# Self attention stage: projections, weighted sums and totals moved to other slots of a group, row maxima two slots further ahead

## The chip, the cores and the metric

One Trainium2 chip, one core. The metric is device time in microseconds of one execution; a median of runs is given. The kernel is one program in which the five engines (TensorE, VectorE, ScalarE, GpSimd, SyncE) each run their own instruction list and wait for each other on semaphores only.

## The reference, cut to what matters

A decoder layer on x of 8 x 512 x 512 with 16 heads of 32: self attention with a second "memory" branch, cross attention against ctx_1024, a small two-expert feed-forward, and a layer norm behind each. The change lies in the self attention alone:

```python
qk = x @ w_attn.T + b_attn              # q and k; v = x
scores = einsum('bhqd,bhkd->bhqk', q, k) * scale   # causal
y_ar = einsum('bhqk,bhkd->bhqd', softmax(scores), v)
k2 = x[:, :-1] @ w_k2.T + b_k2
qa = -leaky_relu(-q2 * scale, 0.02);  ka = sigmoid(k2 * scale * 0.02)
# a later stage: ma = tril(qa ka^T), y_ma = ma @ (v[1:] - y_ar[:-1])
```

## The kernel before, in words

The self stage works on 32 groups (8 batches x 4 groups of 4 heads). A group has 16 slots, numbered 0 to 15 in the texts; `split_slot` gives each as (kt, j): a tile kt of 128 keys and a head j. So slot 4 is (1, 0), slot 11 is (2, 3). Every engine walks the same list of slots, and within a slot it issues what belongs to it in the order of the code. There is no planner; tables and `if` lines on (kt, j) set all of the order.

What TensorE issues in slot n of group g (`self_tensor`):

1. the transposed scores of slot n (L339; 512, 384, 256, 256 columns for kt = 0 to 3). It waits until the exponential of slot n-2 has left one of two PSUM banks, and in slot 0 for the row `self_shift`, the negated row maxima, that a DMA (L759) puts under the stacked q/k operand;
2. plain scores for the row maxima of a slot further ahead (L390 in `self_scores`, SELF_LEAD = 24 slots; 256, 256, 384, 512 columns, by m % 4). They wait for the stacked operand of the group that they belong to (`kq_landed`, the DMAs of L752) and for VectorE's maximum of three slots before (`dve_max`);
3. in slot 11 the weighted sums of key tiles 0 and 1 (L403);
4. at most one projection step: three 512-column matmuls (L203 to L205) of a later group, in 12 slots of 16, by the table PROJECTED. A group's steps are 0 to 3 for q, 4 to 7 for k, 8 to 11 for k2;
5. in slot 3 the weighted sums of tiles 2 and 3 of the group before, and then its totals (L362, into PSUM bank 6);
6. in slot 10, last, the transpose of the next group's row maxima (L378) into bank 6. It waits until VectorE has normalised the group before, which uses bank 6 as well (`dve_norm`).

VectorE in each slot takes the row maximum of slot n + SELF_LEAD (L583), then has: the low part of k (L590, slot 2), the normalisation of the group before (`self_norm`: four reciprocals of 128 columns, L620, in slots 4 to 7, and one multiplication, L626, in slot 8), the low part of the shift (L598, slot 11), and the low part of q and qa (L606, L610, slot 14). ScalarE has the exponential of every slot (L465), the copy of k (L470, slot 1), the copy of y (L483, slot 4), tanh for ka (L478, slot 6), its + 1 (L488, slot 8), a copy for the totals (L493, slot 9), the copy of the shift (L499, slot 11), and q and its relu (L507, L511, slot 13). GpSimd masks each tile's exponentials (L652) and adds them up (L668). SyncE issues all DMAs in order: the stack of 12 for the next-but-one group (L752, slot 5), v, qa, ka, and the shift (L759, slot 12). Bank 7 carries q and k2, bank 6 carries k, totals and the transpose.

Before group 0 there are three groups of slots (g = -3 to -1) in which only projections and maxima are done; group 1's q and k are projected by a second table (SECOND) in slots 1 to 8 of g = -2. From g = 29 on (LATE_NORM) the normalisation comes behind the transpose. Behind the last slot the memory stage and then the cross attention follow.

Of the kernel before, what the change touches and what calls it, by code (L numbers as in the profile page):

```python
# [16 lines left out]
P = 128  # L17
# [19 lines left out]
SELF_MAX = (0, 1, 5)  # L37
CROSS_MAX, CROSS_MAX_FIRST = (1, 0), (0, 1, 7)

SELF_LEAD, CROSS_LEAD = 24, 22  # L40


def split_slot(n):
# [12 lines left out]
def arrive(eng, sem):  # L56

    eng.drain().then_inc(sem, 1)
# [152 lines left out]
class SelfPhase:  # L211
    def __init__(self, nc, ctx, t):
        def sem(name):
# [62 lines left out]

PROJECTED = {(0, 0): (2, 7), (0, 1): (1, 8), (0, 2): (1, 9), (0, 3): (1, 10), (1, 1): (1, 11), (2, 0): (3, 0),
             (2, 1): (3, 1), (2, 2): (3, 2), (3, 0): (3, 3), (3, 1): (3, 4), (3, 2): (3, 5), (3, 3): (3, 6)}  # L280

SECOND = {(0, 1): 0, (0, 2): 1, (0, 3): 2, (1, 0): 3, (1, 1): 4, (1, 2): 5, (1, 3): 6, (2, 0): 7}
SECOND_AT = -2
Q_COPY, Q_LOW, K_COPY, K_LOW, STACK_AT = (3, 1), (3, 2), (0, 1), (0, 2), (1, 1)
SECOND_Q_COPY, SECOND_Q_LOW, SECOND_K_COPY, SECOND_K_LOW, SECOND_STACK = (1, 1), (1, 2), (2, 1), (2, 2), (2, 2)


# [31 lines left out]
def shift_bank(sh, d):  # L319

    return sh.bank[7 if d > LATE_NORM else 6]


def self_tensor(pe, s, second, third, cw, sh):
    pe.wait_ge(sh.const, CONSTS)
    pe.wait_ge(s.pool_ones, 3)
    for n in SELF_SLOTS:
        g, kt, j = split_slot(n)
        if n in ROUND_AT:
            memory_round_tensor(pe, s, second, third, cw, sh, ROUND_AT[n])  # L330
        if 0 <= n < NS:
            first = kt * P
            q0 = min(first, SEQ - 256)
            kq, bank = s.kq[g % 3], sh.bank[2 + n % 2]
            if kt == 0 and j == 0:
                pe.wait_ge(s.shift_landed[g % 3], 32 * (g // 3 + 1))
            if n >= 2:
                pe.wait_ge(s.act_exp, n - 1)
            pe.matmul(bank[:, 0:SEQ - q0], kq[0:98, 1, j, first:first + P], kq[0:98, 0, j, q0:SEQ],  # L339
                      start=True, stop=True).then_inc(s.pe_st, 1)  # L340
        m = n + SELF_LEAD
        if 0 <= m < NS:
            self_scores(pe, s, sh, m)

        if (kt, j) == (2, 3) and 0 <= g < NG:
            self_weighted(pe, s, sh, TILES * g)
            self_weighted(pe, s, sh, TILES * g + 1)
        part = projection_at(g, kt, j)
        if part is not None:
            self_project(pe, s, sh, *part)  # L350
        if kt == 0 and j == 3 and 0 <= g - 1 < NG:
            d = g - 1
            self_weighted(pe, s, sh, TILES * g - 2)
            self_weighted(pe, s, sh, TILES * g - 1)
            pe.wait_ge(s.pool_add, 3 * (d + 1))
            pe.wait_ge(s.act_copied, d + 1)
            pe.wait_ge(s.dve_k, min(d + 4, NG))
            if d + 4 > NG:
                pe.wait_ge(s.dve_sh, min(d + 2, NG))
                pe.wait_ge(s.dve_norm, NORM * d)  # L360
            for jj in range(PER):
                done = pe.matmul(sh.bank[6][rows_of(jj), :], sh.ones[:, :], s.added[:, jj, :],  # L362
                                 start=True, stop=True, skip_group_check=True)
            done.then_inc(s.pe_tot, 1)
        if kt == 2 and j == 2 and 0 <= g + 1 < NG:
            d, n16 = g + 1, PER * TILES
            pe.wait_ge(s.dve_max, n16 * (d + 1))
            if g == LATE_NORM:

                pe.wait_ge(s.act_k2, 2 * (g + 1) + 1)  # L370
            elif g > LATE_NORM:
                pe.wait_ge(s.dve_sh, g + 1)
                pe.wait_ge(s.act_k2, min(2 * (g + 1) + 1, 2 * NG - 1))
            elif g >= 1:
                pe.wait_ge(s.dve_norm, NORM * g)
            else:
                pe.wait_ge(s.dve_k, g + 3)
            pe.transpose(shift_bank(sh, d)[0:n16, 0:P], s.negmax[d % 2][:, :], sh.ident[:, :]).then_inc(s.pe_sh, 1)  # L378
    arrive(pe, sh.self_done)


def self_scores(pe, s, sh, m):
# [57 lines left out]
def self_scalar(act, s, second, third, cw, sh):  # L440
# [6 lines left out]
    for n in SELF_SLOTS:  # L447
        g, kt, j = split_slot(n)
        if g == -2 and kt == 2 and j == 2:
            for i in range(2 * GROUPS, 3 * GROUPS):  # L450
                self_weight_high(act, s, i)
        if n in ROUND_AT:
            memory_round_scalar(act, second, third, cw, sh, ROUND_AT[n])
        if 0 <= n < NS:
            step = n // PER
            first = kt * P
            q0 = min(first, SEQ - 256)
            if j == 0 and step >= 3:
                before = step - 3
                act.wait_ge(s.pe_pv, before + 1)  # L460
                act.wait_ge(s.pool_add, 3 * (before // TILES) + max(before % TILES, 1))
                if before % TILES == 0:
                    act.wait_ge(s.act_copied, before // TILES + 1)
            act.wait_ge(s.pe_st, n + 1)
            act.activation(s.pt[step % 3][:, j, 0:SEQ - first], sh.bank[2 + n % 2][:, first - q0:SEQ - q0], ACT.Exp,  # L465
                           scale=SCALE_SELF).then_inc(s.act_exp, 1)
        d = copied_at(g, kt, j, K_COPY, SECOND_K_COPY, 2)
        if d is not None:
            act.wait_ge(s.pe_k, d + 1)
            act.activation(s.stage[d % 2][:, 2, :].bitcast(F32R), sh.bank[6][:, :], ACT.Identity,  # L470
                           bias=bias_column(s, K, d)).then_inc(s.act_k, 1)
        if kt == 1 and j == 2 and 0 <= g + 1 < NG:
            d = g + 1
            ka = s.memory[:, 1, 1:SEQ]
            act.wait_ge(s.pe_k2, d + 1)
            if d >= 1:
                act.wait_ge(s.ka_stored, 16 * d)
            act.activation(ka, sh.bank[7][:, 0:SEQ - 1], ACT.Tanh, bias=bias_column(s, K2, d), scale=KSCALE).then_inc(s.act_k2, 1)  # L478
        if kt == 1 and j == 0 and 0 <= g - 1 < NG:
            act.wait_ge(s.pe_pv, TILES * g)  # L480
            if g >= 2:
                act.wait_ge(s.dve_norm, NORM * (g - 1))
            act.activation(s.y_raw[:, :], sh.bank[4][:, :], ACT.Copy).then_inc(s.act_raw, 1)  # L483
        if kt == 2 and j == 0 and 0 <= g + 1 < NG:
            d = g + 1
            ka = s.memory[:, 1, 1:SEQ]
            act.wait_ge(s.act_k2, 2 * d + 1)
            act.activation(ka, ka, ACT.Copy, bias=1.0).then_inc(s.act_k2, 1)  # L488
        if kt == 2 and j == 1 and 0 <= g < NG:
            act.wait_ge(s.pool_mask, TILES * g + 1)  # L490
            if g >= 1:
                act.wait_ge(s.pe_tot, g)
            act.activation(s.added[:, :, 0:P], s.pt[TILES * g % 3][:, :, 0:P], ACT.Copy).then_inc(s.act_copied, 1)  # L493
        if kt == 2 and j == 3 and 0 <= g + 1 < NG:
            d = g + 1
            act.wait_ge(s.pe_sh, d + 1)
            if d >= 1:
                act.wait_ge(s.shift_landed[(d - 1) % 3], 32 * ((d - 1) // 3 + 1))
            act.activation(s.shift[:, 0, :].bitcast(F32R), shift_bank(sh, d)[0:PER * TILES, 0:P],  # L499
                           ACT.Copy).then_inc(s.act_sh, 1)  # L500
        d = copied_at(g, kt, j, Q_COPY, SECOND_Q_COPY, 3)
        if d is not None:
            if d >= 2:
                for jj in range(PER):
                    act.wait_ge(s.kq_landed[(d - 2) % 3][jj], 48 * ((d - 2) // 3 + 1))
            act.wait_ge(s.pe_q, d + 1)
            act.activation(s.stage[d % 2][:, 0, :].bitcast(F32R), sh.bank[7][:, :], ACT.Identity,  # L507
                           bias=bias_column(s, Q, d)).then_inc(s.act_q, 1)
            if d >= 1:
                act.wait_ge(s.dve_q, 2 * d)  # L510
            act.activation(s.relu[:, :], sh.bank[7][:, :], ACT.Relu, bias=s.bias_relu[:, d % GROUPS:d % GROUPS + 1],  # L511
                           scale=-RELU).then_inc(s.act_q, 1)
        if next_x(g, kt, j) is not None:
            self_x_high(act, s, next_x(g, kt, j))
# [33 lines left out]
def bias_column(s, which, g):  # L548
    return s.bias[:, which * GROUPS + g % GROUPS:which * GROUPS + g % GROUPS + 1]


def self_vector(dve, s, second, third, cw, sh):
# [15 lines left out]
    for n in SELF_SLOTS:  # L568
# [3 lines left out]
                self_weight_low(dve, s, i)  # L572
        if n in ROUND_AT:
            memory_round_vector(dve, second, third, cw, sh, ROUND_AT[n])
        m = n + SELF_LEAD
        if 0 <= m < NS:
            gm, jm, qt = split_slot(m)
            if jm == 0 and qt == 0 and gm >= 2:
# [11 lines left out]
            dve.scalar_tensor_tensor(out=st[:, 3, :].bitcast(F32R), in0=sh.bank[6][:, :], scalar=bias_column(s, K, d),  # L590
                                     in1=st[:, 2, :], op0=ALU.add, op1=ALU.subtract).then_inc(s.dve_k, 1)
        if 0 <= g - 1 < NG and not LATE_NORM <= g < NG - 1:
            self_norm(dve, s, sh, g - 1, PER * kt + j - PER)
        if kt == 2 and j == 3 and 0 <= g + 1 < NG:
            d = g + 1
            hl = s.shift
# [1828 lines left out]
```

## Time and profile before

| | |
|---|---|
| median of 3 runs | 1758.37 us (1756.82 to 1758.61) |
| profiled execution | 1754.45 us, its span 1752.7 us |
| TensorE busy | 1663.1 us, 95% of the span |
| VectorE, ScalarE, GpSimd busy | 1256.1, 992.1, 1160.6 us |

The span is the time from the first to the last instruction of the profiled execution. A line of the timeline gives the start in us, the duration in us, engine, line and operation; a bracket at its end is the idle time of the engine before it and what ended it. Matmuls overlap: one with 512 columns lasts some 0.4 us but the next can start 0.23 us behind its start, so the distance of starts is what counts. "PEld" is the weight load that goes ahead of a matmul.

### The profile page before, as it was taken

The page shows a single profiled execution, that of the slowest core. Times are in us where ns is not written, and L with a number is a line of the kernel's source. Part 1 is how long each engine was busy: PE and PEld are TensorE (multiplying, and loading weights), DVE is VectorE, ACT ScalarE, POOL GpSimd, SP SyncE. Part 2 cuts the span into 40 slices and gives each one's busy share as a digit, 9 for nine tenths or more (in the row PEclk, how much of TensorE's full clock was granted, in tenths as well). Part 3 has the DMA queues.
Part 4 walks back from the last instruction along what each step waited for, and adds up shares of the span by engine and source line. Part 5 has one row for each costly group of instructions (what it writes and reads, how often), then busy time and mean ns, then how long its engine had stood idle before and what let it go on. Part 6 is the DMA issues. An engine that isn't in the chain of part 4 may idle for free.

```text
span 1752.7 us, 30880 instructions
## 1 busy us (share of the span) xinstructions
PE 1663.1 (95%) x10584; PEld 1097.7 (63%) x10584; DVE 1256.1 (72%) x2786; ACT 992.1 (57%) x2002; POOL 1160.6 (66%) x963
## 2 busy tenths in 40 slices
PE   6999999999999889999998999999999999999998
PEld 4666666666666647877863456566565655656566
DVE  6677777777777656767876786877778687777845
ACT  4555555555555543433445666666666666667564
POOL 1555556556555564745565987969788786888874
PEclk9999999999999989999998999999999999999999
DMA  7566566565555555576625543535344344534210
GB/s 216 136 156 166 140 158 163 144 157 154 155 142 150 139 172 180 186 236 186 192 71 157 146 115 88 139 95 153 91 120 115 85 133 103 140 94 117 64 43 30
DMA packets 172311, 237.80 MB, mean 136 GB/s; under 512 B 22646, under 2 KB 74102, under 8 KB 172156
## 3 DMA queue, kind: packets, MB, share of 16 engines
q1 hardware_dynamic: 172156, 235.84, 49.0%
q8 instruction: 85, 1.39, 0.3%
q14 instruction: 70, 0.57, 0.1%
HBM read 92.10 MB, written 41.94 MB: 76 GB/s over the span
## 4 chain that ended last, share of the span: by engine, by line
PE 67%; DVE 12%; POOL 7%; DMA 5%; issue 3%; SPq 3%; ACT 2%; POOLq 0%; DVEq 0%; ACTq 0%
PE bank L1698 9%; POOL cross_added L2040 5%; PE bank L1567 5%; PE bank L203 5%; PE bank L204 5%; PE bank L1535 5%; PE bank L205 5%; DVE bank L620 5%; PE bank L1506 5%; PE bank L403 4%; PE bank L339 4%; PE bank L390 3%; SPq L752 2%; DVE bank L583 2%; PE bank L1603 2%
## 5 line engine op out<-in xcount | busy, mean ns | idle before, releaser
L1516 DVE TENSOR_REDUCE cross_negmax<-bank 128x1 f32<-128x512 f32 x512 | 338.8, 675 | 132.6 <-PE bank L1506 129.1
L1785 ACT ACTIVATE cpt<-bank 128x512 f32<-128x512 f32 x512 | 297.3, 595 | 122.6 <-PE bank L1535 119.9
L583 DVE CUSTOM_DVE_ANT_0 bank<-bank,future 128x128 f32<-128x128 f32 (+3 forms) x512 | 243.2, 488 | 172.2 <-PE bank L390 171.9
L465 ACT ACTIVATE pt<-bank 128x256 f32<-128x256 f32 (+3 forms) x512 | 217.7, 445 | 261.1 <-PE bank L339 254.9
L2040 POOL TENSOR_TENSOR cross_added<-cross_added,cpt 128x2048 f32<-128x2048 f32 x61 | 280.1, 4591 | 11.4 <-ACT cpt L1785 11.0
L652 POOL TENSOR_SCALAR_AFFINE_SELECT pt<-pt 128x512 f32<-128x512 f32 x128 | 81.1, 634 | 247.0 <-ACT pt L465 246.8
L1535 PE MATMUL bank<-cqk 98*128 98x512 f32 x512 | 225.8, 441 | 10.0 <-ACT cpt L1785 9.5
L1506 PE MATMUL bank<-cqk 96*128 96x512 f32 x512 | 211.6, 417 | 11.0 <-DVE cross_negmax L1516 8.9
L2040 POOL TENSOR_TENSOR cross_added<-cpt,cpt 128x2048 f32<-128x2048 f32 x32 | 146.7, 4585 | 78.1 <-ACT cpt L1785 78.1
L339 PE MATMUL bank<-qk 98*128 98x256 f32 (+2 forms) x512 | 179.2, 355 | 10.5 <-ACT pt L465 4.9
L390 PE MATMUL bank<-qk 96*128 96x256 f32 (+2 forms) x512 | 169.1, 336 | 5.5 <-DVE self_negmax L583 4.4
L203 PE MATMUL bank<-xt_hi,w_hi 128*128 128x512 f32 x384 | 157.4, 410 | 13.0 <-DVE w_lo L541 10.8
L1535 PEld LDWEIGHTS bank<-cqk 98*128 98x128 f32 x512 | 97.0, 190 | 106.0 <-issue 51.2
L204 PE MATMUL bank<-xt_hi,w_lo 128*128 128x512 f32 x384 | 153.7, 400 | 0.0
L339 PEld LDWEIGHTS bank<-qk 98*128 98x128 f32 x512 | 96.3, 189 | 90.6 <-issue 46.9
L205 PE MATMUL bank<-xt_lo,w_hi 128*128 128x512 f32 x384 | 152.4, 397 | 0.0
L1875 DVE RECIPROCAL bank<-bank 128x128 f32<-128x128 f32 x128 | 121.8, 954 | 42.4 <-PE bank L1603 42.4
L1567 PE MATMUL bank<-cpt,cv 128*32 128x512 f32 x1024 | 138.1, 612 | 0.0
L1506 PEld LDWEIGHTS bank<-cqk 96*128 96x128 f32 x512 | 96.0, 189 | 49.8 <-DVE cross_negmax L1516 26.7
L620 DVE RECIPROCAL bank<-bank 128x128 f32<-128x128 f32 x128 | 121.8, 957 | 4.9 <-PE bank L362 4.9
L668 POOL TENSOR_TENSOR self_added<-self_added,pt 128x1024 f32<-128x1024 f32 x64 | 117.4, 1835 | 5.3
L390 PEld LDWEIGHTS bank<-qk 96*128 96x128 f32 x512 | 98.1, 192 | 26.0 <-DVE self_negmax L583 11.5
(210 smaller groups left out, 3619.9 us busy)
## 6 DMA issues: line engine op xcount, KB each, us to landing
qk<-stage SPq DMA_DIRECT2D x384, 128.0 KB, 2.4
cqk<-cstage SPq DMA_DIRECT2D x384, 128.0 KB, 2.3
scratch_memory<-memory SPq DMA_DIRECT2D x64, 256.0 KB, 3.8
ma<-scratch_memory SPq DMA_DIRECT2D x32, 512.0 KB, 4.0
raw<-in_x_t SPq DMA_DIRECT2D x32, 256.0 KB, 2.9
v<-in_x SPq DMA_DIRECT2D x32, 256.0 KB, 3.3
scratch_y_ar<-y_ar SPq DMA_DIRECT2D x32, 256.0 KB, 2.7
my_ar<-scratch_y_ar SPq DMA_DIRECT2D x32, 256.0 KB, 4.5
```

What stands on the lines that cost most here:

```text
L203: pe.matmul(out, a[0], b[0], start=first, stop=False)
L204: pe.matmul(out, a[1], b[0], start=False, stop=False)
L205: return pe.matmul(out, a[0], b[1], start=False, stop=last)
L339: pe.matmul(bank[:, 0:SEQ - q0], kq[0:98, 1, j, first:first + P], kq[0:98, 0, j, q0:SEQ], start=True, stop=True).then_inc(s.pe_st, 1)
L390: pe.matmul(bank[:, 0:max(keys, 256)], kq[0:96, 0, j, tile_of(qt)], kq[0:96, 1, j, 0:max(keys, 256)], start=True, stop=True).then_inc(s.pe ...
L583: dve.tensor_tensor_reduce(out=scores, in0=scores, in1=sh.future[:, SEQ - P * (qt + 1):SEQ], scale=-1.0, scalar=-NEG, op0=ALU.add, op1=ALU ...
L1506: pe.matmul(max_bank(sh, m)[:, :], kq[0:96, 0, jm, tile_of(qt)], kq[0:96, 1, jm, :], start=True, stop=True).then_inc(s.pe_mx, 1)
L1516: dve.reduce_max(s.negmax[gm % 2][:, col:col + 1], max_bank(sh, m)[:, :], AX, negate=True).then_inc(s.dve_max, 1)
L1535: pe.matmul(sh.bank[2 + n % 2][:, :], kq[0:98, 1, j, tile_of(kt)], kq[0:98, 0, j, :], start=True, stop=True).then_inc(s.pe_st, 1)
L1567: done = pe.matmul(sh.bank[4][rows_of(j), :], s.v[g % 2][:, kt, rows_of(j)], s.pt[step % 3][:, j, :], start=(kt == 0), stop=(kt == TILES - ...
L1785: act.activation(s.pt[step % 3][:, j, :], sh.bank[2 + n % 2][:, :], ACT.Exp, scale=SCALE_CROSS).then_inc(s.act_exp, 1)
L2040: pool.tensor_tensor(s.added[:, :, :], old[:, :, :], s.pt[step % 3][:, :, :], ALU.add).then_inc(s.pool_add, 1)
```

## The change

On TensorE: the row-maximum scores run 26 slots ahead instead of 24; the weighted sums of tiles 2 and 3 and the totals go from slot 3 to slot 4 (where there is no projection); the twelve projection steps lie in slots 0 to 3, 5 to 8 and 12 to 15 instead of 0 to 3, 5, 8 to 10 and 12 to 15, so that k ends in slot 15 and no longer in slot 0; the transpose of the maxima is in slot 11, ahead of the weighted sums, and no longer at the end of slot 10. On VectorE: the maxima run 25 slots ahead instead of 24, the normalisation one slot later (5 to 9), the low part of k in slot 1. On ScalarE: k's copy in slot 0, q's in slot 12, tanh ahead of the exponential of slot 4, its + 1 in slot 6, the copy for the totals in slot 7.

```diff
-SELF_LEAD, CROSS_LEAD = 24, 22
+SELF_LEAD, SELF_MAX_LEAD, CROSS_LEAD = 26, 25, 22
-PROJECTED = {(0, 0): (2, 7), (0, 1): (1, 8), (0, 2): (1, 9), (0, 3): (1, 10), (1, 1): (1, 11), (2, 0): (3, 0),
-             (2, 1): (3, 1), (2, 2): (3, 2), (3, 0): (3, 3), (3, 1): (3, 4), (3, 2): (3, 5), (3, 3): (3, 6)}
+PROJECTED = {(0, 0): (1, 8), (0, 1): (1, 9), (0, 2): (1, 10), (0, 3): (1, 11), (1, 1): (3, 0), (1, 2): (3, 1),
+             (1, 3): (3, 2), (2, 0): (3, 3), (3, 0): (3, 4), (3, 1): (3, 5), (3, 2): (3, 6), (3, 3): (3, 7)}
-Q_COPY, Q_LOW, K_COPY, K_LOW, STACK_AT = (3, 1), (3, 2), (0, 1), (0, 2), (1, 1)
+Q_COPY, Q_LOW, K_COPY, K_LOW, STACK_AT = (3, 0), (3, 2), (0, 0), (0, 1), (1, 1)
@@ self_tensor
+        if kt == 2 and j == 3 and 0 <= g + 1 < NG:
+            self_shift(pe, s, sh, g)
         if (kt, j) == (2, 3) and 0 <= g < NG:
             self_weighted(pe, s, sh, TILES * g)
             self_weighted(pe, s, sh, TILES * g + 1)
         part = projection_at(g, kt, j)
         if part is not None:
             self_project(pe, s, sh, *part)
-        if kt == 0 and j == 3 and 0 <= g - 1 < NG:
+        if kt == 1 and j == 0 and 0 <= g - 1 < NG:
...
-        if kt == 2 and j == 2 and 0 <= g + 1 < NG:
...
+def self_shift(pe, s, sh, g):      # the removed block, its waits unchanged
@@ self_scalar
-        if kt == 1 and j == 2 and 0 <= g + 1 < NG:     # tanh, behind the exponential
+        if kt == 1 and j == 0 and 0 <= g + 1 < NG:     # tanh, ahead of the exponential
-        if kt == 2 and j == 0 and 0 <= g + 1 < NG:     # ka + 1
+        if kt == 1 and j == 2 and 0 <= g + 1 < NG:
-        if kt == 2 and j == 1 and 0 <= g < NG:         # copy for the totals
+        if kt == 1 and j == 3 and 0 <= g < NG:
@@ self_vector
-        m = n + SELF_LEAD
+        m = n + SELF_MAX_LEAD
-            self_norm(dve, s, sh, g - 1, PER * kt + j - PER)
+            self_norm(dve, s, sh, g - 1, PER * kt + j - PER - 1)
```

## Rows read from the trace of the kernel before

**Rows 1.** The page, busy time and share of each engine.
```profile
PE 1663.1 (95%) x10584; PEld 1097.7 (63%) x10584; DVE 1256.1 (72%) x2786; ACT 992.1 (57%) x2002; POOL 1160.6 (66%) x963
```

**Rows 2.** Windows: length, busy of PE, PEld, DVE, ACT, POOL, granted clock, DMA.
```profile
28.50:35.50 7.00, 4.56 (x11) 3.51 (x12) 5.47 (x17) 0.00 (x0) 1.09 (x1) 0.51 0.89 204
300.00:600.00 300.00, 289.22 (x1729) 197.04 (x1729) 213.32 (x648) 167.42 (x388) 167.66 (x123) 1.00 0.56 149
608.00:616.00 8.00, 5.47 (x15) 4.45 (x16) 4.40 (x13) 1.81 (x4) 3.45 (x3) 0.57 0.21 64
```

**Rows 3.** Line L378: idle time before it, and who ended it.
```profile
  DVE y_ar L626: 14.4, 28
```

**Rows 4.** Timeline of TensorE, one group: slot 11 to slot 11.
```profile
301.56 0.27 PE L378 MATMUL bank<-ident,self_negmax 128*16 128x128 f32 x1 [0.52 <-DVE y_ar L626]
301.59 0.36 PE L339 MATMUL bank<-qk 98*128 98x256 f32 x1
...
302.12 1.71 PE L403 MATMUL bank<-pt,v 128*32 128x512 f32 x16
...
307.80 0.40 PE L339 MATMUL bank<-qk 98*128 98x512 f32 x1
...
308.15 0.40 PE L203 MATMUL bank<-xt_hi,w_hi 128*128 128x512 f32 x1
308.38 0.40 PE L204 MATMUL bank<-xt_hi,w_lo 128*128 128x512 f32 x1
...
312.27 0.86 PE L403 MATMUL bank<-pt,v 128*32 128x256 f32 x16
312.95 1.04 PE L362 MATMUL bank<-self_added,ones 128*32 128x512 f32 x8
...
314.20 0.28 PE L390 MATMUL bank<-qk 96*128 96x256 f32 x1
...
320.46 0.27 PE L378 MATMUL bank<-ident,self_negmax 128*16 128x128 f32 x1 [0.52 <-DVE y_ar L626]
```

**Rows 5.** Timeline of VectorE in the same group, behind the totals.
```profile
314.52 0.30 DVE L583 CUSTOM_DVE_ANT_0 bank<-bank,future 128x128 f32<-128x128 f32 x1 [2.09 <-PE bank L390]
314.74 0.96 DVE L620 RECIPROCAL bank<-bank 128x128 f32<-128x128 f32 x1
...
319.63 0.68 DVE L626 TENSOR_TENSOR y_ar<-bank,self_y_raw 128x512 f32<-128x512 f32 x1
...
321.74 0.27 DVE L598 TENSOR_TENSOR self_shift<-bank,self_shift 16x128 fp32r<-16x128 f32 x1
```

**Rows 6.** Timeline, stack and shift: VectorE's low part of k, SyncE's issues.
```profile
303.19 1.20 SPq L759 DMA_DIRECT2D qk<-self_shift  x2
...
311.00 0.74 DVE L590 SCALAR_TENSOR_TENSOR stage<-bank,bias,stage 128x512 fp32r<-128x512 f32 x1
...
311.77 7.83 SPq L752 DMA_DIRECT2D qk<-stage  x12
```

**Rows 7.** Waits (us, times, longest); then tile qk: issue to landing of its DMAs.
```profile
PEld bank L339 <- DMA qk<-self_shift: 7.0, 11, 3.0
...
DMA to landing us min/median/max: 1.8/2.4/4.4
```

**Rows 8.** Timeline of group 29, which has few projections: TensorE behind ScalarE.
```profile
606.98 0.39 PE L339 MATMUL bank<-qk 98*128 98x256 f32 x1 [0.61 <-ACT pt L465]
...
610.53 0.79 PE L339 MATMUL bank<-qk 98*128 98x512 f32 x1 [2.63 <-DMA qk<-self_shift]
```

**Rows 9.** Timeline of the start, slots 6 to 14 of g = -2.
```profile
23.81 0.39 PE L390 MATMUL bank<-qk 96*128 96x256 f32 x1
...
24.94 0.69 ACT L470 ACTIVATE stage<-bank,bias 128x512 fp32r<-128x512 f32 x1 [1.84 <-PE bank L205]
...
26.59 3.55 DVE L541 TENSOR_TENSOR w_lo<-pt,w_hi 128x512 fp32r<-128x512 f32 x4
...
30.86 1.99 PE L390 MATMUL bank<-qk 96*128 96x384 f32 x4 [4.36 <-DVE self_negmax L583]
```

More of the change, by code:

```diff
@@ L364, in self_tensor @@
             done.then_inc(s.pe_tot, 1)
-        if kt == 2 and j == 2 and 0 <= g + 1 < NG:
[L366 to L378, printed above, removed]
-    arrive(pe, sh.self_done)
+    arrive(pe, sh.self_done)
+def self_shift(pe, s, sh, g):
+    d, n16 = g + 1, PER * TILES
+    pe.wait_ge(s.dve_max, n16 * (d + 1))
+    if g == LATE_NORM:
+        pe.wait_ge(s.act_k2, 2 * (g + 1) + 1)
+    elif g > LATE_NORM:
+        pe.wait_ge(s.dve_sh, g + 1)
+        pe.wait_ge(s.act_k2, min(2 * (g + 1) + 1, 2 * NG - 1))
+    elif g >= 1:
+        pe.wait_ge(s.dve_norm, NORM * g)
+    else:
+        pe.wait_ge(s.dve_k, g + 3)
+    pe.transpose(shift_bank(sh, d)[0:n16, 0:P], s.negmax[d % 2][:, :], sh.ident[:, :]).then_inc(s.pe_sh, 1)
 def self_scores(pe, s, sh, m):
@@ L453, in self_scalar @@
             memory_round_scalar(act, second, third, cw, sh, ROUND_AT[n])
+        if kt == 1 and j == 0 and 0 <= g + 1 < NG:
+            d = g + 1
+            ka = s.memory[:, 1, 1:SEQ]
+            act.wait_ge(s.pe_k2, d + 1)
+            if d >= 1:
+                act.wait_ge(s.ka_stored, 16 * d)
+            act.activation(ka, sh.bank[7][:, 0:SEQ - 1], ACT.Tanh, bias=bias_column(s, K2, d), scale=KSCALE).then_inc(s.act_k2, 1)
         if 0 <= n < NS:
@@ L471, in self_scalar @@
                            bias=bias_column(s, K, d)).then_inc(s.act_k, 1)
-        if kt == 1 and j == 2 and 0 <= g + 1 < NG:
[L473 to L478, printed above, removed]
         if kt == 1 and j == 0 and 0 <= g - 1 < NG:
```

## The prediction

> **What bounds the kernel now.** The page comes first: TensorE is busy 95% of the span [rows 1], so time can only go where TensorE stands still or its clock is low. The windows say where: from 300 to 600 us, inside the self stage, it is busy 289 of 300 us at full clock [rows 2], and "busy" hides more, since a 512-column matmul is booked with 0.40 us but the next starts 0.23 us behind it [rows 4]. Then the waits at one line: before the transpose L378 it stood 28 times, 14.4 us in all, for VectorE's y_ar L626 [rows 3]. So one group is read closely on the timeline.
>
> The self stage repeats exactly: from one L378 to the next 320.46 - 301.56 = 18.90 us [rows 4], and 28 groups (g = 1 to 28) end in that y_ar wait [rows 3]. I cut a group into three stretches [rows 4]. A: weighted sums in slot 3 to L378, 320.46 - 312.27 = 8.19. B: L378 to the weighted sums of slot 11, 302.12 - 301.56 = 0.56. C: these to the weighted sums of slot 3, 312.27 - 302.12 = 10.15.
>
> Stretch A is set by VectorE, not TensorE. The totals start at 312.95 and end at 313.99, yet the first reciprocal starts at 314.74, because VectorE's list has the maximum of slot 4 ahead of it, whose scores L390 TensorE issues only behind the totals, at 314.20 [rows 4, 5]. From there VectorE has no gap: four reciprocals and four maxima (256, 384, 512, 128 columns) in 319.63 - 314.74 = 4.89, then y_ar, and L378 follows its start after 320.46 - 319.63 = 0.83 [rows 4, 5].
>
> **The change part by part.** *Totals and normalisation one slot later, maxima leads 26 and 25 (stretch A).* Now TensorE issues slot 4's two score matmuls ahead of the weighted sums, and VectorE in slot 5 takes a maximum whose scores were also issued ahead of them. So VectorE is idle and ready when the totals end. It started 0.04 behind the modelled end of L390 (314.20 + 0.28, then 314.52) [rows 4, 5]; I take the same behind the totals: first reciprocal at 313.99 + 0.04 - 312.27 = 1.76 from the start of A, against 2.47 before, 0.71 sooner. The rest of the chain keeps its length: slots 6 to 9 bring maxima of 512, 128, 256 and 384 columns, the same four widths in another order. A = 1.76 + 4.89 + 0.83 = 7.48.
>
> Does TensorE have less work than that in A? Weighted sums up to the totals 0.68 (312.95 - 312.27), totals 0.97 as an upper value (their modelled end is 1.04 behind their start), seven pairs of score matmuls at 0.35 at most (308.15 - 307.80 is the widest transposed one with a 256-column one), four projection steps at 3 x 0.23 = 0.70: 0.68 + 0.97 + 2.1 to 2.45 + 2.8 = 6.6 to 6.9 [rows 4]. VectorE still sets A, and about 0.6 us of the wait before L378 stays.
>
> *The transpose in slot 11 (B).* Slot 11's score pair moves ahead of L378 into A's shadow, and the weighted sums follow at once. B becomes the transpose's own distance and a switch of matmul shape. Bounds 0.03 (L339 started so soon behind L378, 301.59 - 301.56 [rows 4]) and 0.2; I take 0.10. *Stretch C* gains slot 4's pair, 2 x 384 columns: 2 x 0.18 = 0.36 (0.23 x 384/512 each), so 10.51. The sum is 7.48 + 0.10 + 10.51 = 18.09, that is 0.81 less per group, and 28 x 0.81 = 22.7 us.
>
> TensorE's 32-column matmuls (L403, L362) stand between full-width ones. On the way from a full-width matmul into them and back the starts are some 0.1 us further apart than the columns ask, four times a group; 0.10 us is what B has for that. The Trainium skill ("TensorEngine Tiling (Array Packing)", Key Properties) says that a change of tiling mode drains TensorE. L378 has 16 output columns: if it counts as column-tiled, L378 to L403 needs no drain and B is 0.03 instead of 0.10; by that rule the sum would be 2 us lower. No row of before has L378 next to L403.
>
> *Slots without a projection are now 4, 9, 10 and 11.* There TensorE needs 0.24 to 0.35 per slot, while ScalarE must keep two slots behind: group 29, with few projections, shows TensorE waiting 0.61 for it [rows 8]. But there ScalarE has copies between the exponentials; in the new order they are in slots 4 to 7, which have projections (1.05 us per slot: 0.35 + 0.70), and three exponentials alone remain. Even some 0.4 of such waits stays inside the 0.6 of slack in A. I take nothing; upper bound one wait of 0.61 more than the slack, net 0.5 per group.
>
> *Tanh ahead of slot 4's exponential, q in slots 5 to 8.* Its k2 ends in slot 3, and TensorE then has 1.65 us of weighted sums and totals: tanh (0.71 on ScalarE) is covered, and the wait for bank 7 goes. *Exponential of slot 4* now waits for weighted sums issued after it; next needed by slot 6's scores, 2 us on: nothing.
>
> *k one slot sooner.* Projection end, copy, L590 and the stack of 12 DMAs move from slots 0, 1, 2 to 15, 0, 1, at least one slot (1.05 us) sooner than the 311.77 of now [rows 6]. The scores that need its head 0 go from slot 8 to slot 6 of the group. Three issues are 3/12 of 7.83, 1.96, and they land after 2.4 (1.8 to 4.4) [rows 6, 7]. Stack issue, relative to slot 4, goes from -0.4 to at most -1.45, so head 0 is there at about 2.9; slot 6 comes at 0.36 + 1.65 + 1.05 + 0.3 = 3.36. Covered by 0.4; below, the price if not.
>
> *Shift DMA.* L598 ran 1.28 behind L378 and SyncE issued at 1.63 (303.19 - 301.56) because VectorE had the maxima of slots 10 and 11 (384 and 512 columns) between [rows 4 to 6]. Now they have 512 and 128: sooner by some 0.5, issue about 1.1. Slot 0's scores come 0.10 + (307.80 - 302.12 = 5.68) = 5.8 behind L378, against 6.24. Room is 4.7 now, 4.6 before: the waits (7.0 us on the loads, 3.0 of it one case [rows 7]) shrink a little. -1, between -2 and +3.
>
> *SyncE, GpSimd.* SyncE's list keeps its order; the stack ends sooner, so nothing behind it is later. GpSimd's mask and additions have the whole of C as cover; the totals come a slot later for it. Nothing.
>
> *Start.* SELF_LEAD 26 puts the first two L390 in slots 6 and 7 of g = -2, ahead of the projection steps 5 and 6 of group 1, and they wait for group 0's stack, which let L390 go at 23.81 [rows 9]. These two steps (2 x 0.70) and some L390 now come behind 23.81 instead of ahead. On the end of k for group 1 hang the copy (24.94), the low weights (26.59, 3.55 long) and the maxima, for which TensorE then waits 4.36 us [rows 9]. All of that is 1.6 us later; with the first shift having one slot less of cover, +2. While TensorE resumes, the granted clock is 0.51, the lower of its two levels (1.2 GHz) [rows 2]; a longer stop can cost up to 2 more or nothing.
>
> *End.* In group 29 the scores waited 2.63 us for the shift [rows 8], which SyncE issued behind the stack. That stack starts at least 1.05 sooner, and the totals of groups 30 and 31 stand behind one slot less: -2, between 0 and -5. The upper end is the case in which the clock doesn't fall behind that wait; it was 0.57 from 608 to 616 us [rows 2].
>
> Sum: -22.7 - 1 + 2 - 2 = -23.7. The profiled execution took 1754.45 (span 1752.7), which would become 1730.8. The median of runs is 3.9 above it, so 1758.4 - 23.7 = 1734.7; I forecast 1734.5. Cross attention and memory stage have no edit and start as much sooner.
>
> **The rivals.** *ScalarE takes VectorE's place in slots 9 to 11.* The 0.61 of group 29 speaks for it, the exponentials' free run against it. By the bound above, 0.5 of the 0.81 goes: 28 x 0.31 = 8.7, plus the other terms (-1): 1748.7.
>
> *The stack is late for slot 6: slower.* TensorE issues in order, so a late head 0 in slot 6 holds back the projection steps, every later exponential and the totals' successors. It decides from the point at which the landing is 0.81 behind slot 6's scores (it eats the whole gain there), which is a landing 1.2 later than my 2.9. For it: the largest landing of 4.4 is 2.0 above the median [rows 7]. If that were the rule, it would wait 1.6 per group, net +0.8 x 28 = 22, so 1758.4 + 22 - 1 = 1779. At 1.0 of wait it is 1763. Against: 2.4 is the median.
>
> *The gain is given back later.* The memory stage begins with loads that wait for stores and for GpSimd's constants; half is lost: 1746.
>
> *Better.* The wait before L378 goes further than the chain says, since TensorE's work is down to 6.6: up to 0.3 more per group, 1726.
>
> *Nothing.* Another engine's period is already 18.9: 1758. VectorE is busy 213 of 300 us [rows 2], so no.
>
> **How the numbers follow.** Forecast 0.60, with its own range 1730 to 1740; ScalarE 0.11; late stack 0.07; given back 0.10; better 0.07; nothing 0.05. Range 1726 to 1748: it holds forecast, better, given back and the near side of the ScalarE case. What a measurement can tell from no change is about 0.2%, 3.5 us. Faster 0.60 + 0.11 + 0.10 + 0.07 = 0.88, same 0.05, slower 0.07.
>
> **What the changed kernel's profile would show.** Right: L378 every 18.1 us, still ended by y_ar L626, at some 0.5 us; a reciprocal within 0.1 of the totals' end; the first L390 of the start still at 23.8 and the k copy behind it at 26.5. Wrong: waits at L339 for pt L465 in slots 9 to 11, waits at L390 for the stack in slot 6, more than 10 us at L339 for the shift, or a period of 18.9.

## The result, and the profile after

| kernel | median (range, executions) | ratio to before [95%] | profiled execution, span, clock |
|---|---|---|---|
| before | 1758.5 us (1756.8 to 1762.0, 4) | | 1754.45, 1752.7, 0.990 |
| changed | 1738.2 us (1735.7 to 1743.2, 4) | 0.9877 [0.9852, 0.9901] | 1743.17, 1741.4, 0.983 |

The change makes the kernel 20.3 us, 1.2%, faster; 23.9 were forecast. (Beside the experiments the kernel before was timed again, with medians of 1756.6 to 1760.2 us.) The two profiled executions differ by only 11.3 us: that of before was quicker than all of its timed ones in the table, that of after is the slowest of its four. So the traces are compared stage by stage, and the sum is made against the medians. In the accounts "period" is the distance from one transpose of the maxima to the next (median over the self stage), and A, B and C are the stretches of the prediction. Line numbers have shifted: L378 is now L382, L390 L393, L403 L406, L362 L364, L620 L623, L626 L629, L598 L601, L752 L755, L759 L762.

First the page's busy row, then one window (columns as in [rows 2]) of the changed kernel.

```profile
PE 1664.8 (96%) x10584; PEld 1116.3 (64%) x10584; DVE 1257.6 (72%) x2786; ACT 1011.9 (58%) x2002; POOL 1161.0 (67%) x963
```
```profile
300.00:600.00 300.00, 292.86 (x1777) 210.16 (x1775) 223.34 (x672) 183.87 (x403) 172.86 (x132) 0.99 0.57 152
```

TensorE has the same 10584 matmuls and within 0.1% the same busy sum as before [rows 1]; in the 300 us window 1777 of them start where 1729 did [rows 2], 2.8% more work in the same time. Only idle time and spacing changed. Half of the wait shown before the transpose is gone; the same row had 14.4 us [rows 3]:

```profile
  DVE y_ar L629: 7.1, 28
```

One group on TensorE's timeline, slot 11 to slot 11, answers to [rows 4]; below it VectorE behind the totals [rows 5], and SyncE [rows 6].

```profile
295.95 0.27 PE L382 MATMUL bank<-ident,self_negmax 128*16 128x128 f32 x1 [0.26 <-DVE y_ar L629]
296.14 1.71 PE L406 MATMUL bank<-pt,v 128*32 128x512 f32 x16
...
306.17 0.34 PE L339 MATMUL bank<-qk 98*128 98x384 f32 x1
306.34 0.33 PE L393 MATMUL bank<-qk 96*128 96x384 f32 x1
306.61 0.86 PE L406 MATMUL bank<-pt,v 128*32 128x256 f32 x16
307.28 1.04 PE L364 MATMUL bank<-self_added,ones 128*32 128x512 f32 x8
308.25 0.44 PE L339 MATMUL bank<-qk 98*128 98x384 f32 x1
...
314.12 0.27 PE L382 MATMUL bank<-ident,self_negmax 128*16 128x128 f32 x1 [0.25 <-DVE y_ar L629]
```
```profile
308.39 0.97 DVE L623 RECIPROCAL bank<-bank 128x128 f32<-128x128 f32 x1 [1.05 <-PE bank L364]
309.26 0.64 DVE L586 CUSTOM_DVE_ANT_0 bank<-bank,future 128x512 f32<-128x512 f32 x1
...
313.29 0.69 DVE L629 TENSOR_TENSOR y_ar<-bank,self_y_raw 128x512 f32<-128x512 f32 x1
```
```profile
296.92 1.20 SPq L762 DMA_DIRECT2D qk<-self_shift  x2
...
304.30 7.75 SPq L755 DMA_DIRECT2D qk<-stage  x12
```

VectorE now stands idle when the totals end: the reciprocal starts 1.78 behind the weighted sums and nothing stands before it. A is 314.12 - 306.61 = 7.51 (before 8.19), B 296.14 - 295.95 = 0.19, 0.20 as the median (before 0.56), C 10.47 here and 10.49 as the median (before 10.15). The period is 18.20 against 18.90.

The start and group 29 answer to [rows 9] and [rows 8]:

```profile
25.16 0.39 PE L393 MATMUL bank<-qk 96*128 96x256 f32 x1 [1.41 <-DMA qk<-stage]
...
27.94 0.69 ACT L480 ACTIVATE stage<-bank,bias 128x512 fp32r<-128x512 f32 x1 [3.57 <-PE bank L205]
...
29.45 2.48 DVE L544 TENSOR_TENSOR w_lo<-pt,w_hi 128x512 fp32r<-128x512 f32 x4
...
32.26 1.47 PE L393 MATMUL bank<-qk 96*128 96x512 f32 x3 [2.83 <-DVE self_negmax L586]
```
```profile
591.26 0.79 PE L339 MATMUL bank<-qk 98*128 98x512 f32 x1 [2.33 <-DMA qk<-self_shift]
```

By stage, transposes of the profiled executions as marks: the second of them is at 55.45 before and 59.06 after (the program's first projection matmul at 10.84 and 11.78), the thirtieth at 586.69 and 568.88. The 28 groups between take 531.24 and 509.82, 21.4 less. From there to the first memory round it is 55.7 and 56.9; the rest of the program is 1110.3 and 1115.6. A second trace of the same changed kernel (after_again, below) has 55.4 and 1113.4, and in the traces of e1 to e10, whose later stages are the same, the rest takes 1107.7 to 1114.4, so that the 1110.3 of before lies inside. So the gain is the self stage's, and the 5.3 us by which the later stages look longer here belong to this one execution. A row of theirs:

```profile
773.29 0.63 ACT L1731 ACTIVATE cstage<-cstage 128x512 fp32r<-128x512 f32 x1 [11.01 <-DMA cstage<-in_ctx_t]
```

This load's wait was 8.86 before; TensorE then stood 2.99, its granted clock was at the lower level from 774.5 to 781.3 us, and the lead of the changed kernel, 15.8 us at 767 us by the same VectorE instructions in both traces, was 10.8 at 787 us.

### The profile page after: what moved, and what is told of

The parts are those of the page before. It is cut to its first block, busy times and chain, and to the rows that moved or that the text cites. A ratio compares the mean times of both kernels' runs of the same rounds, so it can differ in the third digit from the quotient of the medians.

```text
span 1741.4 us, 30880 instructions
## 1 busy us (share of the span) xinstructions
PE 1664.8 (96%) x10584; PEld 1116.3 (64%) x10584; DVE 1257.6 (72%) x2786; ACT 1011.9 (58%) x2002; POOL 1161.0 (67%) x963
## 4 chain that ended last, share of the span: by engine, by line
PE 68%; DVE 12%; POOL 7%; issue 4%; DMA 4%; SPq 3%; ACT 2%; POOLq 0%; ACTq 0%; DVEq 0%
PE bank L1701 9%; POOL cross_added L2043 6%; PE bank L203 5%; PE bank L204 5%; PE bank L205 5%; PE bank L1570 5%; PE bank L1538 5%; PE bank L1509 5%; PE bank L406 4%; DVE bank L623 4%; PE bank L339 4%; PE bank L393 3%; DVE bank L586 2%; SPq L755 2%; PE bank L1606 2%
## 5 line engine op out<-in xcount | busy, mean ns | idle before, releaser
L475 ACT ACTIVATE pt<-bank 128x256 f32<-128x256 f32 (+3 forms) x512 | 221.8, 438 | 206.5 <-PE bank L339 192.4
L2043 POOL TENSOR_TENSOR cross_added<-cross_added,cpt 128x2048 f32<-128x2048 f32 x61 | 280.0, 4590 | 11.3 <-ACT cpt L1788 10.9
L339 PE MATMUL bank<-qk 98*128 98x256 f32 (+2 forms) x512 | 179.5, 354 | 6.8 <-ACT pt L475 4.0
L393 PE MATMUL bank<-qk 96*128 96x256 f32 (+2 forms) x512 | 169.2, 335 | 5.5 <-DVE self_negmax L586 4.1
L339 PEld LDWEIGHTS bank<-qk 98*128 98x128 f32 x512 | 97.3, 191 | 83.4 <-ACT pt L475 39.7
L623 DVE RECIPROCAL bank<-bank 128x128 f32<-128x128 f32 x128 | 121.9, 957 | 35.7 <-PE bank L364 35.7
L393 PEld LDWEIGHTS bank<-qk 96*128 96x128 f32 x512 | 98.1, 192 | 26.9 <-DVE self_negmax L586 5.3
```

Source lines behind the costliest of these rows:

```text
L393: pe.matmul(bank[:, 0:max(keys, 256)], kq[0:96, 0, j, tile_of(qt)], kq[0:96, 1, j, 0:max(keys, 256)], start=True, stop=True).then_inc(s.pe ...
L2043: pool.tensor_tensor(s.added[:, :, :], old[:, :, :], s.pt[step % 3][:, :, :], ALU.add).then_inc(s.pool_add, 1)
```

## The experiments

The theory: the group's period is A + B + C, A is VectorE's chain hung on the end of the totals (first reciprocal to y_ar), B and C are TensorE's own. Rivals: ScalarE, the projections' places or the stack set it.

### after_again: the changed kernel once more

> The changed kernel once more, as the base for its neighbours on the same chip. Theory (VectorE's chain sets stretch A): L382 every 18.20 us as in its first profile, 1735 to 1743 us. The second question is the clock: its first profile had 59 us at the lower level against 35 us before, and ended 11.3 us ahead of before, while the median is 20.3 ahead. If that was chance, this profile will have another sum of low-clock time and an end that differs by about half of the difference; if the change itself puts TensorE at the lower level, it stays near 0.983 to 0.986 in every run.

1738.2 us (1735.7 to 1740.4), ratio 0.9887 [0.9869, 0.9905]; span 1736.1 at clock 0.988. The medians of A, B, C and the period are the same to 0.01. The clock was at its lower level for 40.8 us in all, against 59.0 in the first trace and 34.4 before, and the span is 5.3 us shorter than in the first, where about 9 were expected. So the low clock of the first trace does not belong to the edit, and no trace shows that the edit makes the later stages slower.

### e1_lead24 and e2_lead24_norm4: the leads

```diff
 e1 and e2
-SELF_LEAD, SELF_MAX_LEAD, CROSS_LEAD = 26, 25, 22
+SELF_LEAD, SELF_MAX_LEAD, CROSS_LEAD = 24, 24, 22
 e2 also
-            self_norm(dve, s, sh, g - 1, PER * kt + j - PER - 1)
+            self_norm(dve, s, sh, g - 1, PER * kt + j - PER)
```


> Both leads back to 24, all else as changed. Theory: VectorE's slot 5 then begins with a maximum whose scores TensorE issues behind the totals, so the first reciprocal comes 0.7 later, as before the change; period 18.20 + 0.71 = 18.9, the start gets its 1.7 back: about 1756 us. Rival (the gain is the new slots of the projections, which take ScalarE's waits away): the period stays at 18.2, about 1736.5 us.

> Both leads at 24 and the normalisation back in slots 4 to 8; totals stay in slot 4. Theory: what VectorE has ahead of the first reciprocal is then the maximum of slot 4, whose scores TensorE issues ahead of the totals; the first reciprocal stays within 0.1 of the totals' end without any lead, period 18.2, and the start gets 1.7 back: about 1736.5 us, perhaps with shift waits of 0.1 to 0.5 per group since three maxima now stand between y_ar and the low part of the shift. Rival (the longer lead itself is needed): period 18.9, about 1756 us.

e1: 1762.2 us, 1.003 [1.0017, 1.0043], period 19.11, A 8.32, C 10.58: slower than the kernel before, and 6 us and 0.2 of period above the forecast. The maximum of the slot with the first reciprocal waits again for scores issued behind the totals, and TensorE's wait before the transpose grows from 0.25 to 1.11:

```profile
319.21 0.43 DVE L586 CUSTOM_DVE_ANT_0 bank<-bank,future 128x256 f32<-128x256 f32 x1 [1.79 <-PE bank L393]
...
319.56 0.96 DVE L623 RECIPROCAL bank<-bank 128x128 f32<-128x128 f32 x1
```
```profile
325.28 0.27 PE L382 MATMUL bank<-ident,self_negmax 128*16 128x128 f32 x1 [1.11 <-DVE y_ar L629]
```

e2: 1738.8 us, 0.9896 [0.9877, 0.9915], period 18.29, A 7.52. With the normalisation in slots 4 to 8 the old leads do almost as well: A is the same, C is 10.58 as in e1, 0.09 more than with the long leads, for a reason that was not looked into, and the medians are not apart. For A, what counts is not how far ahead the maxima run, but that nothing in VectorE's list between the totals' issue and the first reciprocal needs a matmul issued behind the totals. For A, the long leads are only the price of the normalisation's later slot.

### e5_before_totals4: one part alone, on the kernel before

```diff
-        if kt == 0 and j == 3 and 0 <= g - 1 < NG:
+        if kt == 1 and j == 0 and 0 <= g - 1 < NG:     # weighted sums of tiles 2, 3 and totals
```


> The kernel before with one edit: weighted sums of tiles 2 and 3 and totals in slot 4 instead of 3. Theory: the first reciprocal comes 0.71 sooner, A = 7.48, B stays 0.56 (slot 11's scores come behind the transpose), C = 10.15 + 0.30 for slot 4's pair = 10.45; period 18.49, 28 x 0.41 = 11.5 us less than before: 1747 us. Rival (projections' slots and lead are the gain): 18.9, 1758 us.

1748.2 us, 0.9935 [0.9914, 0.9957]; A 7.51, B 0.56, C 10.45, period 18.52. One line of the diff brings the whole of A's gain, and half of the 20 us.

### e6_transpose10: the transpose back at the end of slot 10

> The changed kernel with the transpose back at the end of slot 10. Theory: the transpose still waits for y_ar, so A stays 7.5, and slot 11's pair of scores comes behind it: B = 0.56 instead of 0.20, period 18.56, 28 x 0.36 = 10 us more: 1748 us. Rival (its place does not matter, since TensorE has slack there): 18.2, 1738 us.

1743.0 us, 0.9904 [0.9889, 0.9919], period 18.44: A and C as in the changed kernel, B 0.44. The transpose's move is worth 0.24 per group, 6.7 us by the period; the medians are 4.8 apart, half of the 10 that were expected. B is 0.44 and not 0.56 because with the lead of 26 the row-maximum score matmul of slot 11 has 256 columns, where with the lead of 24 it has 512 (L390 at 301.79, L403 at 302.12, 0.33 apart; here 0.21):

```profile
297.44 0.27 PE L382 MATMUL bank<-ident,self_negmax 128*16 128x128 f32 x1 [0.91 <-DVE y_ar L629]
297.46 0.36 PE L339 MATMUL bank<-qk 98*128 98x256 f32 x1
297.67 0.28 PE L393 MATMUL bank<-qk 96*128 96x256 f32 x1
297.87 0.64 PE L406 MATMUL bank<-pt,v 128*32 128x512 f32 x4
```

### e4_proj_back: the projections and ScalarE's copies back

The table PROJECTED, the slots of k's and q's copies, of tanh, of its + 1 and of the totals' copy as in the kernel before; the rest changed.

> Projections, k and q copies, tanh, ka + 1 and the copy for the totals back in their old slots; leads 26 and 25, totals in slot 4, normalisation in 5 to 9 and transpose in 11 stay. Theory: stretch A stays VectorE's, 7.5 us; k's stack starts a slot and more later, so the scores of slot 6 wait for head 0, up to 0.6, which the slack in A still holds: period 18.2 to 18.5, 1738 to 1747 us. Rival (the slots of the projections are the gain): 18.8 or more, 1755 us or above.

1741.6 us, 0.9899 [0.9883, 0.9916]; period 18.20. The medians are 3.3 us apart, the intervals overlap. The period doesn't need this part. In the trace four of the 28 groups are 0.2 to 0.8 us longer than the period, 1.8 us in all (changed kernel: 0.2), three of them by a late shift; and there are more waits for the exponential (changed kernel: 4.0 us in 12) and the stack (1.4 in 1):

```profile
PE bank L339 <- ACT pt L468: 9.1, 40, 0.6
PE bank L393 <- DMA qk<-stage: 3.5, 3, 1.4
```

### e3_start_held: the first three row-maximum scores held until slot 8

```diff
-        if 0 <= m < NS:
+        if 2 < m < NS:
             self_scores(pe, s, sh, m)
+        elif m == 2:
+            for early in range(3):
+                self_scores(pe, s, sh, early)
```


> The changed kernel with the first two row-maximum scores of the start held back to slot 8 of g = -2, where they were before, so that the projection steps 5 and 6 of group 1 are not behind them. Theory: k's copy of group 1 at about 1.6 us earlier against the stack's start, all later work too, period unchanged 18.20: 1736.5 us. Rival (the start's 2 us came from the weights' loads, which vary from run to run): no difference, 1738 us.

1736.0 us (1731.9 to 1743.3), 0.9876 [0.9854, 0.9898]. The interval overlaps that of the changed kernel, so the gain is not shown. In the trace the low weights came 0.8 us sooner (28.15 against 28.82 in after_again, counted from the first projection matmul 16.76 against 17.56), but the second transpose did not (46.57 against 46.44 from there). What eats the 0.8 us is open.

### e7_totals_first and e8_half_reciprocal: what sets A

```diff
 e7, self_tensor, slot 4
-            self_weighted(pe, s, sh, TILES * g - 2)
-            self_weighted(pe, s, sh, TILES * g - 1)
             pe.wait_ge(s.pool_add, 3 * (d + 1))
             ...                                       # the totals
+            self_weighted(pe, s, sh, TILES * g - 2)
+            self_weighted(pe, s, sh, TILES * g - 1)
 e8, self_norm
-        sums = sh.bank[6][:, tile_of(k)]
+        sums = sh.bank[6][:, P * k:P * k + P // 2]
```


> The changed kernel with the totals ahead of the weighted sums in slot 4 instead of behind them. If VectorE's chain from the totals' end to y_ar sets stretch A (6.84 us from the first totals matmul to the transpose, in every variant so far), the transpose comes 0.68 us sooner, until TensorE's own work (it waits 0.52 before the transpose now) takes over: 0.5 to 0.68 per group, 28 groups, 14 to 19 us: 1720 to 1724 us. Rival (A is no more than the sum of TensorE's and ScalarE's work, and the chain only happens to end there): the exponential of slot 4 and the copy of y come 0.97 us later, no gain or a loss, 1738 us or more.

> The changed kernel with each of the four reciprocals over 64 of its 128 columns; the other half of the sums is left as it is. It measures the chain by its length. Theory (VectorE sets A): the chain is some 4 x 0.4 = 1.6 us shorter, so A falls from 7.51 to TensorE's own work, 6.9 to 7.0, period 17.6 to 17.7, 28 x 0.5 to 0.6 = 14 to 17 us: 1721 to 1724 us. Rival: A stays 7.51 and the transpose waits for something else (the maxima, or the exponentials of slots 9 to 11), 1738 us.

e8, which leaves half of the sums without their reciprocal and so serves to measure only: 1721.0 us, 0.9786 [0.9765, 0.9808], period 17.64, and no wait before the transpose at all: less work on VectorE alone takes 0.56 from A (now 6.95). So in the changed kernel VectorE sets A. A reciprocal of half the columns, against 0.96 for the whole:

```profile
301.97 0.56 DVE L623 RECIPROCAL bank<-bank 128x64 f32<-128x64 f32 x1
```

The 6.95 are not TensorE's work alone. In slot 11 the weight load of L339 waits for ScalarE's exponential, here and, at 313.21, in the changed kernel as well:

```profile
305.60 0.19 PEld L339 LDWEIGHTS bank<-qk 98*128 98x128 f32 x1 [0.21 <-ACT pt L475]
```
```profile
305.31 0.28 PE L393 MATMUL bank<-qk 96*128 96x256 f32 x1
305.60 0.39 PE L339 MATMUL bank<-qk 98*128 98x256 f32 x1
305.82 0.29 PE L393 MATMUL bank<-qk 96*128 96x256 f32 x1
305.95 0.27 PE L382 MATMUL bank<-ident,self_negmax 128*16 128x128 f32 x1
306.15 0.64 PE L406 MATMUL bank<-pt,v 128*32 128x512 f32 x4
```

The starts are 0.29 and 0.22 apart where a 256-column matmul takes 0.12 elsewhere. That is 0.27 of the 6.95, and 6.68 without it. The row of PE shows no wait there, because the modelled end of a matmul hides it.

e7: 1730.4 us, 0.9842 [0.9825, 0.9859], period 17.97: 0.23 less where 0.5 to 0.7 was expected. Two timelines, VectorE and TensorE, show why:

```profile
305.18 0.97 DVE L623 RECIPROCAL bank<-bank 128x128 f32<-128x128 f32 x1 [0.40 <-PE bank L362]
306.40 0.70 DVE L586 CUSTOM_DVE_ANT_0 bank<-bank,future 128x512 f32<-128x512 f32 x1 [0.26 <-PE bank L393]
...
307.02 0.96 DVE L623 RECIPROCAL bank<-bank 128x128 f32<-128x128 f32 x1
```
```profile
304.04 1.06 PE L362 MATMUL bank<-self_added,ones 128*32 128x512 f32 x8
304.93 0.83 PE L406 MATMUL bank<-pt,v 128*32 128x256 f32 x16
305.69 0.44 PE L339 MATMUL bank<-qk 98*128 98x384 f32 x1
305.97 0.40 PE L393 MATMUL bank<-qk 96*128 96x512 f32 x1
```

The first reciprocal is early, but the maximum behind it waits for scores at 305.97, now behind the weighted sums. The old wait has come back one place further on.

### e9_two_reciprocals and e10_two_reciprocals_only: the version that this points to

```diff
-            self_norm(dve, s, sh, g - 1, PER * kt + j - PER - 1)
+            k = PER * kt + j - PER - 1
+            if k == 0:
+                self_norm(dve, s, sh, g - 1, 0)
+            if k >= 0:
+                self_norm(dve, s, sh, g - 1, k + 1)
```
e9 has this and e7's edit, e10 this alone.

> Two edits: the totals ahead of the weighted sums in slot 4 (as in the run before with that edit alone, period 17.97 us), and the first two reciprocals both in VectorE's slot 5, ahead of the maximum of slot 6, with the third, the fourth and y_ar still in slots 6, 7 and 8. Theory: in the run with the totals first VectorE lost time because the maximum of slot 6 waits for scores L390 that TensorE issues behind the weighted sums; with a second reciprocal (0.96) between, these scores are there when the maximum comes, VectorE has no gap from the totals to y_ar, and the period falls to some 17.7, TensorE's own floor being 17.64 by the run with half reciprocals: about 1723 us. Rival: VectorE's slots 9 to 11, behind y_ar, or the buffers of the maxima set the period, and it stays at 17.97, 1730 us.

> The changed kernel with only the first two reciprocals taken together in VectorE's slot 5 (the totals stay behind the weighted sums). Theory: VectorE has no gap between the totals and y_ar there in the changed kernel, so another order of the same work gives nothing: A 7.51, period 18.20, 1738 us. Rival: the maxima come later, TensorE's scores L390 wait for their buffers, and the period grows by up to the 0.96 of one reciprocal.

e9: 1723.6 us (1721.3 to 1726.6), 0.9816 [0.9800, 0.9833], period 17.73. The theory held: VectorE has no gap from the totals on, and no wait stands before the transpose.

```profile
301.97 1.78 DVE L627 RECIPROCAL bank<-bank 128x128 f32<-128x128 f32 x2 [0.40 <-PE bank L362]
303.65 0.64 DVE L586 CUSTOM_DVE_ANT_0 bank<-bank,future 128x512 f32<-128x512 f32 x1
```
```profile
307.88 0.27 PE L382 MATMUL bank<-ident,self_negmax 128*16 128x128 f32 x1
```

e10: 1744.0 us, 0.9936 [0.9920, 0.9953], period 18.38. Here the rival came true, though smaller than its bound. y_ar is ready sooner (4.42 behind the first reciprocal, not 4.90, with one maximum less ahead of it), but the maxima behind it are later, and TensorE's scores wait for their buffer, 17.6 us in 32 over the run:

```profile
309.41 1.78 DVE L627 RECIPROCAL bank<-bank 128x128 f32<-128x128 f32 x2 [1.05 <-PE bank L364]
...
313.83 0.69 DVE L633 TENSOR_TENSOR y_ar<-bank,self_y_raw 128x512 f32<-128x512 f32 x1
```
```profile
315.10 0.38 PE L393 MATMUL bank<-qk 96*128 96x256 f32 x1 [0.48 <-DVE self_negmax L586]
315.32 0.27 PE L382 MATMUL bank<-ident,self_negmax 128*16 128x128 f32 x1
```

A is 7.69, and the transpose comes 1.49 behind y_ar's start and no longer 0.83. So y_ar is not the only thing of VectorE that A hangs on; the maxima of the same slots come next. With the totals first (e9) both are early enough.

## Why the prediction was right, and where it was off

**Stretch A: right.** Forecast 1.76 + 4.89 + 0.83 = 7.48; the rows above give 1.78 (308.39 - 306.61), 4.90 and 0.83, 7.51. e8 confirms that VectorE sets it, and its 6.95, or 6.68 without what ScalarE adds, stands against 6.6 to 6.9. The slack is so 7.51 - 6.95 = 0.56, as forecast (about 0.6), though the profile shows a wait of 0.25 and not the 0.5 that was named as a sign: it counts from the modelled end of a matmul. e5 shows that the slot of the totals alone does it.

**Stretch B: the term that was mis-sized.** 0.10 was taken, 0.20 came, the upper bound, 2.8 us in 28 groups. The prediction said that B is the transpose's own distance and a switch of matmul shape. For the switch it took the 0.10 of the edges between full-width and 32-column matmuls, and that size is right: in e7 L406 to the next matmul takes 0.76 (305.69 - 304.93), and 0.67 in the changed kernel, where 32-column totals follow, which is 0.09. For the transpose itself it took nothing, since L339 starts 0.03 behind it [rows 4]. But one start further on the trace of before has

```profile
301.79 0.40 PE L390 MATMUL bank<-qk 96*128 96x512 f32 x1
```

0.20 behind L339 (301.79 - 301.59), where a 256-column matmul takes 0.12 elsewhere. TensorE had just waited there, and a matmul behind a wait also has 0.22 without any transpose (e8, 305.82 - 305.60), so this row can't tell the transpose's share. e8 and e6 can: from a 256-column L393 to the weighted sums it takes 0.33 with the transpose between (306.15 - 305.82, no wait), and 0.21 without it (297.87 - 297.67, 0.21 before rounding). The transpose adds 0.12, and 0.12 and 0.09 make the measured 0.20. This is worked out from these rows; no run was made for it. The reading by which L378 counts as column-tiled and needs no drain gave 0.03; the 0.20 speaks against it, since the same 0.09 is left beside the transpose's own time as at the other edges. That a change of tiling mode drains TensorE (the Trainium skill, "TensorEngine Tiling (Array Packing)", Key Properties) agrees with it if the 16-column transpose is not in the mode of the 32-column tiles.

**Stretch C: right.** 10.51 forecast, 10.49.

**The period** was so 18.20 instead of 18.09: 0.70 less, 28 x 0.70 = 19.6 instead of 22.7. That is most of the difference between forecast and result. The experiments show that the period carries the time: 28 times a kernel's difference in period to the changed kernel, added to 1738.2, gives the medians of e1 to e10, all ten, within 3.4 us (e9: 1725.0 against 1723.6; e1: 1763.7 against 1762.2; e4, the farthest: 1738.2 against 1741.6).

**Shift: right, a little small.** SyncE issued 0.97 behind the transpose (296.92 - 295.95) where 1.1 was forecast and 1.63 was before [rows 6]. The groups' excess over the median period, which falls in groups that wait for a late shift, fell from 2.0 us in all to 0.2: -1.8 against -1.

**Start: right.** +2 forecast. From the first projection matmul to the second transpose it is 44.61 before, 47.28 and 46.44 after: +2.7 and +1.8. The way was the forecast one, with k's copy 2.1 later against the first projection matmul where 1.6 were forecast: first row-maximum scores at 25.16, k's copy at 27.94, low weights at 29.45, all late by the two projection steps behind the stack's wait. Of these times 0.94 is the later first matmul of this execution. The wait of 4.36 [rows 9] became three, 1.41 + 0.61 + 2.83. Both forecast parts can be seen. The first transpose is 29.99 behind the first projection matmul before, 30.3 in e1 and e5, which have the old leads as well, and 31.4 to 32.5 in all kernels with the long ones; but e2 has the old leads and 32.2, so executions differ here by as much as the part is worth. And from the first transpose to slot 0 of group 0, where the shift has less cover, it takes 4.07 before, 5.05 and 4.53 in the two traces of after and 5.04 in e1. So the size is supported by the traces and not shown by a run (e3's gain is not shown either).

**End: wrong, and small.** -2 forecast, nothing found. The step itself happened: in group 29 SyncE issued the shift 1.87 behind the transpose, where before it was 4.26 (607.30 - 603.04):

```profile
584.97 0.28 PE L382 MATMUL bank<-ident,self_negmax 128*16 128x128 f32 x1
```
```profile
586.84 1.83 SPq L762 DMA_DIRECT2D qk<-self_shift  x2
```

But the scores still waited 2.33 (before 2.63 [rows 8]): from issue to scores it took 4.42 (591.26 - 586.84) against 3.23 (610.53 - 607.30). In after_again it took 3.23 again, and there the issue came only 3.40 behind the transpose. So transpose to scores fell from 7.49 to 6.29 and 6.63, and the group, from its slot 0 to the next, became 1.1 and 0.8 us shorter, little more than the 0.7 of every group. Behind it the gain doesn't last: the last transpose to the first memory round takes 20.17 before, 21.57 after and 19.68 in after_again, with the same wait of 0.77 at its end, while the granted clock from 610 to 620 us was 0.71, 0.53 and 0.67. In all, thirtieth transpose to first round: 55.7 before, 56.9 and 55.4 after, and 54.6 to 58.0 in the other kernels. What places the stretches of low clock was not settled.

**The sum**, by what was measured: -19.6 - 1.8 + 2.2 + 0 = -19.2, against -20.3 between the medians. The forecast of -23.7 was too large by 3.1 in the period (2.8 of it B), 2 at the end and 0.2 at the start; the shift gave 0.8 back. The 1.1 between -19.2 and -20.3 is less than the medians can tell.

**The rivals.** ScalarE in slots 9 to 11: it does not set the period, which falls to 17.64 with VectorE out of the way (e8), and TensorE's matmuls L339 wait for its exponential 4.0 us in 12 cases where before had 4.9 in 10. But it is there, as the prediction's own reasoning had it: at the weight loads of L339 the waits for it grew from 20.1 us in 44 cases to 39.7 in 74, one of 0.21 in slot 11 of the group shown, and the slack in A covers them. Once VectorE is faster (e8) they count, with 0.27 per group. The late stack: no; it is issued 1.87 ahead of slot 4 (306.17 - 304.30, forecast at least 1.45), and L393 waits for it once, at the start. Given back later: no, the rest of the program in the traces of all kernels overlaps that of before. Better: no, A has exactly the length of VectorE's chain. Nothing: no. What was missing among them was the small one, the transpose's own time in B.

## What to carry to other kernels

When two engines' lists run in lockstep, write down for each instruction of the waiting engine which instruction of the other it needs, and ask what was issued ahead of that one. Here the whole gain of stretch A came from one maximum that stood before a reciprocal and needed scores issued behind the totals (e5), its undoing from the same (e1), and the next gain was half lost to the same thing one place on (e7) until a reciprocal was put between (e9). A cost of 0.1 us at an edge, 28 times over, is as large as the terms that one worries about at start and end: take it from a row with the same pair of shapes, or keep its whole spread in the sum. And measure an instruction's cost over two starts, with and without it: the start of the next one alone showed 0.03 for a transpose that adds 0.12.

## What the runs showed of the hardware

- From a 16-column transpose (L382) to 32-column matmuls (L406) it takes 0.20 us from start to start, in every kernel that has the pair, whether TensorE waited before it or not (e8: 305.95 to 306.15). Between a 256-column matmul and the 32-column ones the transpose adds 0.12 (e8 against e6). A change between full-width and 32-column matmuls costs 0.09.
- A reciprocal of 64 columns took VectorE 0.56, one of 128 columns 0.96: 0.40 for 64 columns and, if the time is linear in the columns, 0.16 besides (two widths only).
- A wait of TensorE can stand at the weight load alone and be missing at the matmul: 0.21 at L339's load, none in its row of PE (e8, slot 11).
- The same two DMAs of the shift took 3.23 or 4.42 from issue to the scores that wait for them, in two traces of the same kernel; 0.63 of the difference is their issue, which took 1.20 or 1.83.
- The same program's spans differed by 5.3 us (1741.4 and 1736.1) at granted clocks of 0.983 and 0.988, with the median period of the self stage equal to 0.01 us: profiles of one execution can't tell what the medians tell.
